# A six-stage transformer kernel: score maxima carried inside the turned queries, part of the mixtures' preparation on GpSimd, and a layer norm taken in two parts

## The reference, cut to what matters

```python
x = x + 0.5 * ffn0(layernorm(x)); x = x + attn0(layernorm(x)); x = x + 0.5 * ffn0(layernorm(x))
x = x + 0.5 * ffn1(layernorm(x)); x = x + attn1(layernorm(x)); x = x + 0.5 * ffn1(layernorm(x))

# ffn0, for 2048 tokens of 128: the 8 best of 64 experts, at most 64 tokens to an expert
logits = x @ router_w.T
topk_w, topk_ids = top_k(softmax(logits), 8)
pos = cumsum(onehot(topk_ids))[...] - 1          # a token's slot at its expert
routed = sum over its experts with pos < 64 of weight * (silu(x @ w_gate) * (x @ w_up)) @ w_down
out = routed + silu(x @ ws_gate) * (x @ ws_up) @ ws_down          # the shared expert

# attn0, for each of 8 batches of 256 tokens, 16 heads of width 8
q, k = rope(elu(q) + 1), rope(elu(k) + 1)
out = softmax(q @ k.T / sqrt(8)) @ v + depthwise convolution of v over 3 tokens

# attn1, for 4 x 128 tokens and then as before, 16 heads of width 64
logits = Q @ K.T / 8 + mask + R @ D              # R = x @ Wr + br, 10 numbers a head
out = (softmax(logits) @ V) @ Wproj + bproj
```

## Time and profile before

| what | before |
|---|---|
| three timed runs, us | 1099.80, 1115.09, 1109.68; median 1109.68 |
| the profiled execution, us | 1098.92 |
| its span, first to last instruction, us | 1097.2 |
| PE busy | 914.0 us, 83% of the span |
| PE weight loads | 688.1 us, 63% |
| DVE busy | 757.6 us, 69% |
| ACT busy | 534.7 us, 49% |
| POOL busy | 272.2 us, 25% |

### The profile page before, as it was taken

How to read it: one execution, slowest core, us unless ns; L and a number is a source line. 1 busy time by engine, 2 the same in 40 slices (tenths; PEclk the granted TensorE clock), 3 DMA queues, 4 the chain that set the end, 5 groups by cost and what they waited for, 6 DMA issues and landing times.

```text
span 1097.2 us, 23131 instructions
## 1 busy us (share of the span) xinstructions
PE 914.0 (83%) x7238; PEld 688.1 (63%) x7242; DVE 757.6 (69%) x2659; ACT 534.7 (49%) x1489; POOL 272.2 (25%) x349
## 2 busy tenths in 40 slices
PE   5899758999996899937997289999999999658992
PEld 4466646666764456836896166666666766437992
DVE  7767885787868766885555557677677667674555
ACT  4222132665664232034454258677778668523553
POOL 1012183323101004047744410000000000067642
PEclk9999965999996999957999589999999999958997
DMA  9031099600006212083311175534643541253303
GB/s 243 19 98 34 16 364 328 206 2 1 1 2 169 55 41 90 1 249 99 106 42 40 56 211 174 149 113 125 193 116 98 174 135 59 62 153 92 91 32 118
DMA packets 134947, 119.47 MB, mean 109 GB/s; under 512 B 11011, under 2 KB 115227, under 8 KB 134836
## 3 DMA queue, kind: packets, MB, share of 16 engines
q1 hardware_dynamic: 130292, 109.57, 33.9%
q0 software_dynamic: 4544, 8.54, 2.4%
HBM read 67.19 MB, written 51.80 MB: 108 GB/s over the span
## 4 chain that ended last, share of the span: by engine, by line
PE 58%; DVE 21%; issue 9%; DMA 3%; ACT 3%; POOL 3%; SPq 1%; DVEq 1%; POOLq 0%; ACTq 0%
PE psum L802 5%; PE psum L1374 5%; PE psum L1292 4%; PE psum L811 4%; PE psum L1948 4%; PE psum L1997 3%; PE psum L590 3%; PE psum L2418 3%; PE psum L2463 3%; PE psum L2430 2%; DVE a_L L2588 2%; PE psum L592 2%; PE psum L591 2%; DVE a_G L2507 2%; PE psum L1912 2%
## 5 line engine op out<-in xcount | busy, mean ns | idle before, releaser
L2128 DVE TENSOR_REDUCE a_negmax<-psum 128x2 f32<-128x512 f32 x128 | 84.4, 687 | 36.4 <-PE psum L1948 35.6
L2077 ACT ACTIVATE a_PT<-psum 128x1024 f32<-128x1024 f32 x64 | 65.6, 1025 | 28.5 <-PE psum L1980 28.3
L2534 ACT ACTIVATE a_pr<-a_L,a_least 128x128 f32<-128x128 f32 x128 | 50.8, 397 | 54.1 <-DVE a_least L2588 54.1
L857 ACT ACTIVATE f_hT<-psum,f_wt 128x128 f32<-128x128 f32 x156 | 44.7, 369 | 46.8 <-PE psum L802 46.8
L857 ACT ACTIVATE g_hT<-psum,g_wt 128x128 f32<-128x128 f32 x156 | 44.5, 370 | 44.7 <-PE psum L802 40.9
L1948 PE MATMUL psum<-a_turned 24*128 24x256 f32 x256 | 59.3, 355 | 5.7 <-DVE a_negmax L2128 5.7
L2536 ACT ACTIVATE a_pr<-a_L,a_least 128x256 f32<-128x256 f32 x128 | 63.7, 498 | 0.0
L2418 PE MATMUL psum<-a_KT,a_Q 64*128 64x128 f32 (+1 forms) x512 | 59.7, 351 | 1.4 <-DVE a_least L2588 1.4
L2453 PEld LDWEIGHTS psum<-a_PT,a_V 128*64 128x64 f32 x512 | 31.0, 136 | 40.9 <-issue 16.8
L2544 ACT ACTIVATE a_PT<-psum 128x384 f32<-128x384 f32 x128 | 55.6, 489 | 1.9 <-PE psum L2430 1.7
L2430 PE MATMUL psum<-ident,a_pr 128*128 128x128 f32 x384 | 53.6, 276 | 2.9 <-DVE a_pr L2354 2.6
(11 more groups left out here) (574 smaller groups left out, 2687.6 us busy)
## 6 DMA issues: line engine op xcount, KB each, us to landing
z<-a_G SPq DMA_DIRECT2D x32, 512.0 KB, 2.9
a_X<-z SPq DMA_DIRECT2D x16, 1024.0 KB, 7.0
f_slots_dram<-empty SPq DMA_DIRECT2D x1, 8910.0 KB, 27.1
g_slots_dram<-empty SPq DMA_DIRECT2D x1, 8910.0 KB, 51.1
a_X<-z SPq DMA_DIRECT2D x16, 512.0 KB, 3.9
f_wgu<-in_gate_up SPq DMA_DIRECT2D x16, 384.0 KB, 6.3
z<-pad SPq DMA_DIRECT2D x6, 1024.0 KB, 10.3
g_wgu<-in_gate_up SPq DMA_DIRECT2D x16, 384.0 KB, 7.0
```

Of the source, the lines that this page charges most:

```text
L857: act.activation(hT[:, i % 2, c, :], bank[i % 2][:, P * c:P * c + P], ACT.Relu, bias=wt[i % WBUF][:, B1 + c:B1 + c + 1]).then_inc(relu_don ...
L2077: act.activation(PT[m % 4][:, :, :, :].rearrange("p j t n -> p j (t n)"), core.psum[:, 2 + 2 * (u % 2):4 + 2 * (u % 2), :], ACT.Exp, scale ...
L2128: dve.tensor_reduce(negmax[:, :, h], bank[h % 2].rearrange("p (t n) -> p t n", n=SEQ), AX.X, ALU.max, negate=True).then_inc(max_done, 1)
```

## The change

It has three parts.

1. **First attention.** Each head's field of 32 columns now has two own columns ahead of its 24 (OWN = 2, USED = 26): zero in q, one in k. `split_maxima` writes its high and its rest part for each head in these two positions of `mparts`, which has the layout of turned queries (4 groups of 4 x 32) and is otherwise zero. PE turns it in eight transposes (four groups, two halves of the tokens). `take_shift` is no more a copy but an addition of the 128x1024 result into the turned q. The scores by key are then 26 rows of one product; `head`, `select`, `shift` and their semaphores are gone.
2. **Routed mixtures, f and g.** The second halves of `xpart` are computed by GpSimd in two operations a quarter (multiply into `raised`, which lies in the buffer `XT`, then subtract) and the two copies of the slot numbers go there too. PE reads the counts ahead of the zeros. DVE gates the shared expert's fourth quarter between the two halves of the gather and not ahead of them.
3. **Second attention.** The layer norm has functions for the statistics and the roots of any tiles; the first quarter is taken by itself, then normalised. DVE takes the statistics of the others behind that, their roots behind the store of the first piece. GpSimd splits the first batch ahead of the second quarter's normalisation, which waits for the second roots.

```diff
@@ LayerNorm
+    def take_moments(self, dve, tiles):
+        for t in range(tiles.start, tiles.stop):
...
+    def take_roots(self, dve, tiles, n):
+        for t in range(tiles.start, tiles.stop):
             last = dve.bn_aggr(self.mean_var[:, t, :], self.moments[:, t, :])
...
+        self.step(dve, dve.tensor_tensor(rstd, rstd, t, ALU.mult))
+        dve.sem_inc(self.roots_ready, 1)
@@ mixture_zero, gpsimd
+        for q in range(4):
+            tiles = slice(4 * q, 4 * q + 4)
+            pool.wait_ge(ln.xn_ready, 4 * (q + 1))
+            pool.tensor_scalar(raised[:, tiles, :], ln.xn[:, tiles, :], RAISED_X, None, ALU.mult).then_inc(x_raised, 1)
+            pool.wait_ge(x_high, q + 1)
+            pool.wait_ge(x_raised, q + 1)
+            pool.tensor_tensor(xpart[:, 1, tiles, :], raised[:, tiles, :], xpart[:, 0, tiles, :],
+                               ALU.subtract).then_inc(x_cut, 1)
+        pool.wait_ge(loaded, 64)
+        for e in range(2):
+            pool.tensor_copy(number[:, e, :, :], bcast(number_loaded[:, :], WP)).then_inc(spread, 1)
@@ mixture_zero, vector
-        for q in range(4):
-            dve.wait_ge(x_high, q + 1)
-            tiles = slice(4 * q, 4 * q + 4)
-            dve.scalar_tensor_tensor(xpart[:, 1, tiles, :], ln.xn[:, tiles, :], RAISED_X, xpart[:, 0, tiles, :],
-                                     ALU.mult, ALU.subtract).then_inc(x_cut, 1)
...
-        for q in range(4):
+        for q in range(3):
             if q == 2:
                 dve.wait_ge(w_cut, 2)
             shared_hidden(q)
+        dve.wait_ge(spread, 2)
...
         for half in range(2):
             if half:
+                shared_hidden(3)
@@ attention_zero, tensor
-            for t in range(2):
-                last = pe.transpose(bank[T].bitcast(BF16)[:, P * t:P * t + P],
-                                    mparts[:, t, :, :].rearrange("p i h -> p (i h)"), core.identb[:, :])
+            for g in range(GROUPS):
+                for t in range(2):
+                    last = pe.transpose(bank[T].bitcast(BF16)[:, SEQ * g + P * t:SEQ * g + P * t + P], mparts[:, t, g, :],
+                                        core.identb[:, :])
...
-                for j in range(2):
-                    h = 2 * u + j
-                    rows = slice(HW * (h % HG), HW * (h % HG) + HW)
-                    last = pe.matmul(bank[2 + 2 * (u % 2) + j][:, SEQ * t:SEQ * t + SEQ], select[rows, h, :],
-                                     shift[b % 2][rows, :], start=False, stop=True, skip_group_check=True)
@@ attention_zero, vector
-            full = negmax[:, :, :].unsqueeze(2).to_broadcast([P, 2, 4, H0])
-            dve.tensor_copy(mparts[:, :, :, 0:H0], full).then_inc(hi_ready, 1)
+            own = mparts[:, :, :, :].rearrange("p t g (j c) -> p t (g j) c", c=HW)
+            dve.tensor_copy(own[:, :, :, 0], negmax[:, :, :]).then_inc(hi_ready, 1)
...
         def take_shift(b):
             dve.wait_ge(parts_turned, b + 1)
-            if b >= 2:
-                dve.wait_ge(s2_done, STEPS * (b - 1))
-            dve.tensor_copy(shift[b % 2][:, :], bank[T].bitcast(BF16)[:, 0:SEQ]).then_inc(shift_ready, 1)
+            q = turned[b % NT][0]
+            dve.tensor_tensor(q[:, :, :].bitcast(F32R), q[:, :, :], bank[T].bitcast(BF16).rearrange("p (g n) -> p g n", n=SEQ),
+                              ALU.add).then_inc(shift_ready, 1)
@@ attention_one, gpsimd
-        pool.wait_ge(ln.xn_ready, 4)
+        split(0)
+        pool.wait_ge(ln.roots_ready, 2)
         ln.normalise(pool, 1)
-        split(0)
         split(1)
@@ attention_one, vector
-        ln.statistics(dve)
+        ln.take_moments(dve, QUARTER)
+        ln.take_roots(dve, QUARTER, 0)
         ln.normalise(dve, 0)
+        ln.take_moments(dve, OTHERS)
...
-        for k in FIRST:
+        for n, k in enumerate(FIRST):
             if not by_act(k):
                 store_piece(dve, False, 0, k)
+            if not n:
+                ln.take_roots(dve, OTHERS, 1)
```

112 lines of the change are left out of this document (53 added, 59 removed).

## The result

Over 20 runs of each kernel the changed one takes 1109.9 us in the median (1106.5 to 1114.9) and the kernel before 1105.1 us (1096.3 to 1115.7). The ratio is 1.0066, with a 95% interval of 1.0039 to 1.0093. The forecast was 1098 us in a range of 1085 to 1109, as a gain of 7.6 us on what the runs of before stood at. The time is just outside the range, on its slow side, and the sign is wrong, though the change stays within the 2% to which the forecast gave a chance of 0.80.

A forecast was written before the change was run, and what follows sets the result against it. First attention bound by PE in a batch's first steps and DVE in its last; second attention's PE waits for normalised input. Terms -2, -1.5 and -4.1 make -7.6 us, from a mean of 1105.9 to 1098 us; range 1085 to 1109.

The forecast's parts named there:

- the sum of part 1: First attention: savings on PE against longer work on DVE, over all batches, about -2 us.
- The bounds of part 1: First attention: the upper bound, with 2.25 us per shift addition, made it +6.2 us instead of -2.
- The addition: First attention: adding the shift on DVE over 128x1024 from PSUM takes 1.23 us, 0.95 more per batch than the copy.
- rival 2: First attention: the shift addition costs DVE 2.25 us, each batch is 1.1 us longer, the whole 1106 us; chance 12%.
- Net 0.0 us a batch: First attention, five steady batches: 0.8 us gained in three steps, 0.83 lost up to the shift's end.
- Rival 1: First attention: PE bounds it everywhere, so the whole 17 us come and the time is 1083 us; chance 12%.
- The late batches: First attention: the sixth batch changes by -0.3 us, the seventh by about -0.6, the eighth by -1.9.
- Part 2: Beginnings of both routed mixtures: 2.4 us won, 0.5 us per mixture charged for GpSimd blocking DVE, about -1.5 us.
- the loads: Routed mixtures: moving PE's loads of the counts and one gating starts the gather products 1.25 and 1.15 us earlier.
- rival 4: Routed mixtures: GpSimd holds DVE out for whole operations during normalisation, some 5 us late in each, 1108 us; chance 8%.
- Part 3: Second attention: norming the first quarter first brings the first product 5.3 us earlier, of which 4.1 us remain.
- Rival 3: Second attention: the first quarter gains little, through PE's half clock or delayed stores, -1.5 us, time 1101 us; chance 15%.

The follow-up runs named there:

- part 1 alone: Only the first attention's change, on the kernel before: 1149.2 us in the median, against 1136.4 for the kernel before on the same chip.
- b_loads_only: The kernel before with only the loads of the counts and one gating moved in the routed mixtures, nothing given to GpSimd: 1136.1 us, ratio 0.999.
- part 3 alone: Only the second attention's change, on the kernel before: 1139.0 us in the median, ratio 1.0001.

## Why the prediction was wrong, step by step

**The step that failed** is the one that is not in the text: the sum of part 1 took PE's clock in the first attention as given, full from 195 us on as in the one trace of before. It weighed the clock only in part 3. Taking work from PE and making it stand longer in the same batch cost the early rise, some 10 us in the marks up to 235 us (and the dip at 315 to 325, in which the seventh batch took 16.73 us from shift to shift instead of 14.33). The stage's +13.0 us is made of these marks: +9.7 up to the third shift, +1.1 in the next three batches, +0.4 in the sixth, +2.4 in the seventh, -0.6 behind it. The bounds of part 1 went to +6.2 and not beyond, because all of them were made of durations at full clock. The three timed runs of before (1099.8, 1109.7, 1115.1) already held both groups; I read them as spread and added them up to a mean.

**The addition** was right: 1.21 us for 1.23. So rival 2, that it costs 2.25, is out. (Its own sum was loose: 2.25 - 1.23 is 1.02 a batch and not 1.1, and 5.7, 1 and 1 make 7.7 where 8.2 was added.) The steady batch, timeline of DVE after:

```profile
243.23 0.69 DVE L2134 TENSOR_REDUCE a_negmax<-psum 128x2 f32<-128x512 f32 x1 [1.51 <-PE psum L1962]
...
249.42 1.29 DVE L2134 TENSOR_REDUCE a_negmax<-psum 128x2 f32<-128x512 f32 x2 [0.48 <-PE psum L1962]
...
251.98 0.24 DVE L2144 CAST a_mparts<-a_negmax 128x32 bf16<-128x32 f32 x1
...
256.02 1.21 DVE L2152 TENSOR_TENSOR a_turned<-a_turned,psum 128x1024 fp32r<-128x1024 f32 x1
```

and its windows row:

```profile
243.23:263.96 20.73, 18.11 (x184) 13.00 (x182) 17.02 (x38) 11.78 (x15) 6.75 (x9) 1.00 0.01 2
```

**Net 0.0 us a batch** was mis-sized: the period is 20.73 us for 20.35, +0.38. PE's busy time fell by 1.1 us and DVE's rose by 0.85; the forecast had 2 and 0.8. From maximum to maximum, 243.23 to 249.42, three steps took 6.19 us instead of 6.73: 0.54 saved and not 0.8, since in the middle one of them DVE is never idle, so only two steps could gain. The split of the maxima saved nothing (0.24 us for 0.23 before), where I had taken 0.12. The chain from the shift to the maximum stayed at 6.7 us as forecast (257.23 to 263.96). **Rival 1**, PE bounds everywhere, fell with this: at full clock the batch got longer.

**The late batches**: the sixth took 18.15 us for 17.77, +0.4 where -0.3 was forecast; the eighth and what follows it, from shift to next stage, 16.6 instead of 17.2, -0.6 with an addition 0.9 longer, so its steps gave 1.5 of the 1.9. The seventh took 15.14 us at full clock in the trace of part 1 alone (320.85 to 335.99), +0.8 where -0.6 was forecast. So at full clock throughout, part 1 would have cost some 3 us instead of winning 2 (an estimate from these rows: 0.9 ahead of the steady batches, 5 x 0.38, 0.4, 0.8 and -0.6).

**Part 2**: the loads gave what they had (the wait of 1.40 us ahead of the first product is gone, and in b_loads_only that product is 1.1 us earlier), GpSimd took more than that back. The forecast charged 0.5 us a mixture; at the second group of eight best alone it is 1.84, and the first product is 0.5 us late in f and 1.0 in g (33.1 us behind the stage's start for 32.1). This is **rival 4** in a weaker form, at 8%: the normalisation lengthened by 3.5 us and not 7.6, and PE turns the last quarter at 17.82 instead of 17.30. The path went through DVE: its normalisation (+3.51), the operation over 128x8 (+0.86) and the first mask (+0.96) make 5.3 us, against which stand the 2.9 us of work taken from it and the 0.47 us that it used to wait for PE. That leaves 1.9, near the 1.84. The forecast had counted the 2.9 as worth nothing, and had looked for GpSimd's cost in the masks and sums behind the second group of eight best, which kept their length (0.43 and 0.69 us); it lay ahead of them. The Trainium skill (SBUF — State Buffer, Who interferes with whom) says that of DVE and GpSimd, which share a pair of ports, whoever comes second is fully blocked for the other's whole instruction. The 128x8 operation of 1.03 us and the mask of 1.39 agree; the 16 normalisations, 7.70 us instead of 4.19 beside some five operations of GpSimd of 1.2 to 1.5 us each, show that DVE also gets its turns between them, so the price of two whole operations a quarter was too high.

**Part 3** was right in the terms that can be read from the trace after:

```profile
625.15 0.87 DVE L525 BATCH_NORM_STATS2 a_moments<-x 128x6 f32<-128x128 f32 x4 [0.31 <-DVEq L2674]
...
628.03 1.11 DVE L547 TENSOR_SCALAR a_xn<-x,a_mean_var,a_rstd 128x128 f32<-128x128 f32 x4 [0.15 <-DVE a_rstd L541]
...
631.73 0.51 PE L603 MATMUL psum<-a_xs_high,early_wr_rest 128*104 128x256 f32 x1 [2.05 <-POOL a_xs_rest L594]
...
636.82 3.13 POOL L547 TENSOR_SCALAR a_xn<-x,a_mean_var,a_rstd 128x128 f32<-128x128 f32 x4 [5.24 <-DVEq L542]
...
647.12 0.60 PE L553 MATMUL psum<-ident,a_xn 128*128 128x128 f32 x4
```

The first product comes 6.58 us after the statistics begin (11.68 in the earlier trace rows, forecast 6.5), the last quarter is turned at 21.97 (26.08, forecast 22), 4.1 us earlier as forecast. The stage is 3.2 us shorter here and stood at 333.8 to 335.5 in six traces with part 3 on the other chips, at 338.9 to 341.6 in the seven without it; the groups of part 3 alone say 4.5 and 6.6. **Rival 3** is out.

## What to carry to other kernels

Before a sum is made against one trace, look whether the runs fall in groups and find the stage in which they part; a gain that is forecast from one of them is not a gain over the median. Work taken from PE is not worth its busy time where another engine bounds the step, and where the clock in that stretch has two courses it can cost the better one: ask of each removed product what PE does in its place, and of each longer wait whether it falls into the stretch in which the clock still has to rise. Move work to GpSimd beside DVE only where DVE reads PSUM or waits; here small SBUF operations on the path paid a whole GpSimd operation each.
